# A two-layer graph attention kernel: the tail of its attention written by hand, its gates as SILU on ACT, and rows of its output stage loaded ahead

## What is computed

```python
def gt_layer(x, ntype, etype, src, dst, Wk, Wq, Wv, Wa, Watt, Wmsg, pri, skip, g, b):
    k, q, v = (typed_linear(x, ntype, W).reshape(n, H, HS) for W in (Wk, Wq, Wv))
    kT = einsum('nhd,htdo->nhto', k, Watt)
    vT = einsum('nhd,htdo->nhto', v, Wmsg)
    a = einsum('ehd,ehd->eh', kT[src, :, etype], q[dst]) * pri[:, etype].T / SQRT_D
    att = edge_softmax(a, dst, n)
    hag = segment_sum(vT[src, :, etype] * att[:, :, None], dst)
    h = silu(typed_linear(hag, ntype, Wa))
    alpha = sigmoid(skip[ntype])[:, None]
    h = h * alpha + x * (1.0 - alpha)
    return layernorm(h) * g + b          # 8 heads of 16; 16 node types, 32 edge types
out = layernorm(x + (gt_layer(gt_layer(x)) @ ff_w + ff_b))
```

## Time and profile before

| | us |
|---|---|
| median of 3 runs | 3545.18 (3544.02 to 3546.11) |
| profiled execution, its own time | 3543.11 |
| its span in the profile | 3541.3 |
| DVE busy | 2760.1 (78%) |
| PE busy | 2444.9 (69%) |
| POOL busy | 2417.9 (68%) |
| ACT busy | 1910.8 (54%) |

### The profile page before, as it was taken

The page is one execution under the profiler, slowest core; times in us unless marked ns, Lnnn a source line. Parts: engine busy times, 40 slices in busy tenths (PEclk is TensorE's granted clock), DMA queues, the critical chain, the costliest instruction groups (busy, mean ns, idle before and its releaser), DMA issues.

```text
span 3541.3 us, 62787 instructions
## 1 busy us (share of the span) xinstructions
PE 2444.9 (69%) x14287; PEld 1787.5 (50%) x14288; DVE 2760.1 (78%) x6215; ACT 1910.8 (54%) x4886; POOL 2417.9 (68%) x2501
## 2 busy tenths in 40 slices
PE   2777787477667676777677777657667676767765
PEld 1333333366656665666333333346556666666643
DVE  7667677488888888897687888758888787888765
ACT  1666677155445445555576777615445454455555
POOL 3666675577777777773566666477777777777746
PEclk8889998588898989988799999868888888888866
DMA  7999999755555555555799999965555555555350
GB/s 153 399 390 390 379 380 407 250 152 154 151 156 151 152 149 144 147 147 156 193 408 383 389 375 371 412 181 145 146 143 144 144 144 143 145 142 149 95 154 34
DMA packets 331225, 783.39 MB, mean 221 GB/s; under 512 B 87275, under 2 KB 262267, under 8 KB 318335
## 3 DMA queue, kind: packets, MB, share of 16 engines
q0 software_dynamic: 106016, 638.52, 50.7%
q1 hardware_dynamic: 216371, 139.98, 15.0%
q10 hardware_dynamic: 8448, 0.53, 0.2%
HBM read 335.84 MB, written 573.22 MB: 257 GB/s over the span
## 4 chain that ended last, share of the span: by engine, by line
issue 21%; DMA 19%; POOL 18%; DVE 15%; PE 10%; DVEq 9%; ACT 6%; POOLq 1%; SPq 0%; ACTq 0%
POOL region L838 15%; DMA relation_table<-region,scatter_node 13%; DVEq L1901 5%; PE bank L1182 4%; DMA region<-relation_table,key_of 3%; ACT region L925 3%; DVEq L1909 2%; DVE region_q L1879 2%; DVE region L1894 2%; PE bank L1350 2%; DMA region_q<-sums_by_node,gather_node 1%; PE bank L1212 1%; POOL region_q L741 1%; POOLq L831 1%; DVE arena L1884 1%
## 5 line engine op out<-in xcount | busy, mean ns | idle before, releaser
L838 POOL DMA_INDIRECT region<-relation_table,key_of x1568 | 1513.6, 965 | 500.9 <-issue 446.9
L1350 PE MATMUL bank<-region,arena 128*128 128x136 f32 x3968 | 700.3, 329 | 289.8 <-DVE region L1894 157.8
L1350 PEld LDWEIGHTS bank<-region,arena 128*128 128x128 f32 x3968 | 602.8, 226 | 371.5 <-issue 202.2
L925 ACT COPY region<-bank 128x512 f32<-128x512 f32 x1152 | 621.5, 601 | 290.1 <-DMA relation_table<-region,scatter_node 168.9
L1696 DVE COPY region<-bank 128x512 f32<-128x512 f32 x896 | 585.4, 685 | 210.5 <-DMA relation_table<-region,scatter_node 118.4
L1182 PE MATMUL bank<-sums,arena 128*128 128x512 bf16 x2048 | 618.2, 414 | 176.7 <-ACT region L925 142.4
L1061 ACT ACTIVATE arena<-iota_free,minus_dst 128x128 f32<-128x128 f32 x1984 | 629.4, 387 | 153.1 <-PE bank L1350 144.5
L1338 PE MATMUL bank<-region_q 128*128 x3968 | 632.4, 313 | 77.7 <-DVE region_q L1879 54.1
L1338 PEld LDWEIGHTS bank<-region_q 128*128 128x128 f32 x3968 | 596.0, 229 | 84.3 <-issue 84.1
L1870 DVE TENSOR_TENSOR bank<-bank,region 128x512 f32<-128x512 f32 x496 | 345.5, 697 | 292.4 <-issue 177.6
L1079 ACT ACTIVATE bank<-arena 128x256 f32<-128x256 f32 x62 | 24.0, 387 | 911.5 <-DVE arena L1989 911.5
(11 more groups left out here) (303 smaller groups left out, 2911.5 us busy)
## 6 DMA issues: line engine op xcount, KB each, us to landing
arena<-edge_places SPq DMA_DIRECT2D x496, 128.0 KB
region<-relation_table,key_of POOLq DMA_INDIRECT x1568
arena<-segment_flags SPq DMA_DIRECT2D x124, 128.0 KB
region_q<-q_rows SPq DMA_DIRECT2D x6, 768.0 KB, 16.0
aggregated_rows<-one_less_alpha SPq DMA_DIRECT2D x17, 256.0 KB
region<-aggregated_rows SPq DMA_DIRECT2D x16, 272.0 KB, 3.0
sums<-relation_weight_parts SPq DMA_DIRECT2D x32, 128.0 KB, 10.0
x_sorted<-arena SPq DMA_DIRECT2D x16, 256.0 KB, 14.7
```

The costliest lines, as they stand in the source:

```text
L838: pool.indirect_dma_start(out=rows[:, r, s], out_offset=None, in_=table, in_offset=bass.IndirectOffsetOnAxis(ap=key_of[:, n:n + 1], axis=0 ...
L925: nc.scalar.copy(stage[:, r, :, k * HS:(k + 1) * HS], bank[TABLE_BANK + k % TABLE_BANKS][:, :].rearrange("p (t o) -> p t o", t=RT)).then_i ...
L1350: ins = nc.tensor.matmul(bank[SUM_BANK[place_of(block_, q, SUM_RING)]][:, 0:SUMC], onehots[:, at, s], weighed_rows[:, weighed_at, s, :], s ...
```

## The change

It has three parts, and some lines that follow from them.

- The number of quads becomes 244. Block 30 has four, and behind its last product DVE, ACT and PE run a `tail` that is written out: the same helpers in an order of their own. In the tail DVE makes the marks of every second quad from 233 on, with one operation of 128x512 and a semaphore of its own. The last block keeps its differences in the unused half of `score` and its exponentials in the bank of the q rows. The count of early tiles in layer 0 is read by SP instead of POOL.
- ACT's gate is SILU of z. DVE's operation that opened the gate goes in both stages, `half_alpha` becomes `alpha_of_tile`, and `z_used` is replaced by `silu_done` or `var_ready`. In the table stage of layer 1 DVE's variance and centring of the first groups move.
- The first eight groups of h and x rows are loaded as soon as the last quad is weighed, before SP waits for the stored sums, and ACT scales those of h before its first step; the first eight transfers of aggregated rows have the ring's semaphore for themselves.

```diff
-NQUADS = NBLOCKS * QPB
+NQUADS = EDGE_QUADS + NTILES - 1
+LAST_BLOCK = NBLOCKS - 1
+TAIL = (LAST_BLOCK - 1) * QPB
+DVE_MARKS = range(TAIL + 1, NQUADS, 2)
...
+        def below_of(block_):
+
+            return score[:, 1 - block_.par] if block_.known and block_.b == LAST_BLOCK else below_max[:, :, :]
+
+        def exp_bank(block_):
+
+            return Q_BANK[0] if block_.known and block_.b == LAST_BLOCK else EXP_BANK
...
-            return 48 * (g // RING) + 48
+            return 48 * (g // RING) + 16
...
-                    for into, rows_ in ((o_in, agg_dram), (o_res, h_sorted), (o_x, x_sorted)):
-                        sp.dma_start(into[:, k], group_rows(rows_, g)).then_inc(rows_loaded[k], 16)
-
+                    sp.dma_start(o_in[:, k], group_rows(agg_dram, g)).then_inc(rows_loaded[k], 16)
+                    if g >= RING:
+                        for into, rows_ in ((o_res, h_sorted), (o_x, x_sorted)):
+                            sp.dma_start(into[:, k], group_rows(rows_, g)).then_inc(rows_loaded[k], 16)
+
+                sp.wait_ge(weighted, L * NQUADS)
+                for g in range(RING):
+                    for into, rows_ in ((o_res, h_sorted), (o_x, x_sorted)):
+                        sp.dma_start(into[:, g], group_rows(rows_, g)).then_inc(early_rows, 16)
                 sp.wait_ge(agg_stored, AGG_DONE)
...
-                    sp.wait_ge(sums_early, 1)
+                    early_done = sp.value_load(slots_done[0:1, 0:1], min_val=FIRST_LATE, max_val=NQUADS)
+                    sp.wait_ge(sum_added, early_done)
+                    sp.sem_inc(passed, 1)
...
-                    wait(act, z_used, tile.g)
-                    nc.scalar.activation(g_th, by_tile(bank[IN_BANK]), ACT.Tanh, scale=0.5).then_inc(tanh_done, 1)
+                    wait(act, var_ready, tile.g)
+                    nc.scalar.activation(g_th, by_tile(bank[IN_BANK]), ACT.Silu).then_inc(silu_done, 1)
...
+                for g in range(RING):
+                    scale_o_res(g)
                 for i in range(-3, GROUPS + 2):
...
                     if real(i + 3):
-                        scale_o_res(i + 3)
+                        if i + 3 >= RING:
+                            scale_o_res(i + 3)
                         gate(i + 3)
...
+                def tail():
+
+                    for n in range(TAIL, NQUADS):
+                        if n == TAIL:
+                            block_exponentials(Block(0, LAST_BLOCK - 1))
+                        if n == TAIL + 5:
+                            block_exponentials(Block(0, LAST_BLOCK))
+                        block_, q = pair(n)
+                        exponentials(block_, q)
...
+                        if n not in DVE_MARKS:
+                            mark(block_, q)
...
+                    for q in range(4):
+                        turn_maxima(last, q)
+                        sum_quad(*pair(TAIL + 1 + q))
+                    for n in range(TAIL + 5, TAIL + 8):
+                        sum_quad(*pair(n))
+                    spread_rescale(last)
+                    for n in range(TAIL + 8, NQUADS):
+                        sum_quad(*pair(n))
...
-                def open_gate(tile):
-
-                    z = bank[IN_BANK][:, :].rearrange("p (t d) -> p t d", t=GROUP)
-                    wait(dve, hn_ready, tile.g)
-                    dve.wait_ge(tanh_done, tile.g + 1)
-                    v.scalar_tensor_tensor(g_h, g_th, 1.0, z, ALU.add, ALU.mult).then_inc(z_used, 1)
-
...
-                        chain.step(v.scalar_tensor_tensor(hh[:, t], hh[:, t], half_alpha[:, g * GROUP + t:g * GROUP + t + 1], res[:, t],
+                        chain.step(v.scalar_tensor_tensor(hh[:, t], g_th[:, t], alpha_of_tile[:, g * GROUP + t:g * GROUP + t + 1], res[:, t],
...
+                    if l and tile.j == 2 and late.real:
+                        add_res(late, 0)
+                    if l and tile.j == 3 and late.real and tile.n >= 0:
+                        variance(late)
+                    if l and tile.n == 0:
+                        centre(early)
                     if l and tile.j == 0 and early.real:
                         scale(early)
-                    if l and tile.j == 2 and late.real:
-                        add_res(late, 0)
-                    if l and tile.j == 3 and late.real:
-                        variance(late)
...
                     if l and tile.j == 2 and late.real:
                         add_res(late, 1)
+                        if tile.n < 0:
+                            variance(late)
                     if tile.real:
                         evict(tile, DVE_HEADS[6:])
-                    if l and tile.j == 3 and late.real:
+                    if l and tile.j == 3 and late.real and tile.n != -1:
                         centre(late)
...
-                    z = bank[Z_BANK[g % 2]][:, :].rearrange("p (t d) -> p t d", t=GROUP)
                     hh, res = o_h[:, g % 3], o_res[:, g % RING]
...
-                    v.scalar_tensor_tensor(hh, o_th[:, g % 2], 1.0, z, ALU.add, ALU.mult).then_inc(z_used, 1)
...
+                def mark(n):
+
+                    dve.wait_ge(sum_psum, l * NQUADS + n - (ONEHOT_RING - 1))
+                    v.scalar_tensor_tensor(onehots[:, n % ONEHOT_RING], bc(iota_free[:, :], 1, QUAD), -1.0,
+                                           bc(minus_dst[:, n * QUAD:(n + 1) * QUAD], 2, P), ALU.mult, ALU.is_equal).then_inc(dve_marked, 1)
+
+                def tail():
+
+                    before, last = Block(0, LAST_BLOCK - 1), Block(0, LAST_BLOCK)
+                    find_maxima(before, 4, 0)
+                    find_maxima(before, 4, 1)
+                    tail_add(TAIL - 2)
+                    tail_weigh(TAIL)
+                    find_maxima(last, 0, 1)
+                    find_maxima(before, 4, 3)
+                    tail_add(TAIL - 1)
+                    find_maxima(last, 0, 3)
+                    scale_crossing(before.b, tail_tile(TAIL))
+                    find_maxima(last, 0, 0)
...
+                    for n in range(TAIL + 9, NQUADS):
+                        tail_weigh(n)
+                        tail_add(n - 1)
+                    tail_add(NQUADS - 1)
...
-                for at in range(2 + TURN * TURNS, NBLOCKS + 1):
+                for at in range(2 + TURN * TURNS, NBLOCKS):
                     block_of(Block(0, at))
-                for q in range(FIRST_ADDED):
-                    step(Block(0, NBLOCKS + 1), q)
+                tail()
```

165 lines of the change are left out of this document (113 added, 52 removed).

## The result

| | before | after |
|---|---|---|
| median, seven runs each | 3545.18 us (3542.47 to 3547.93) | 3528.16 us (3517.81 to 3532.21) |
| profiled execution, its own time | 3543.11 | 3517.81 |
| its span | 3541.3 | 3516.0 |

The ratio is 0.9945, interval 0.9936 to 0.9954: faster by 17.0 us in the medians and inside the forecast range. The profiled execution of after is its fastest run; five later runs gave 3522.48 (3522.15 to 3523.67; kernel before beside them 3545.08), 22.6 us faster. The seven runs of after spread more than the others: three took 3517.81 to 3522.06 us and four 3528.16 to 3532.21, and none of the five later ones came near the four. No profile of one of the four exists, so what made them longer stays open, and so do 5.7 us of the first median.

The account below looks back on a forecast made before the run. It took table stores, POOL's gathers in attention and an output loop of POOL and DVE, sometimes waiting for TensorE, as bounds. 11.9 + 3.7 + 2.5 + 1.4 + 8 = 27.5 us off 3545.2 gave 3517.7, range 3505 to 3532.

Parts of the forecast that it names:

- (c): Attention and output stage: the changes cancel, leaving little more than layer 0's drain, within 0.2%; chance 0.04.
- (d): Gates: SILU's tables lack COPY or IDENTITY, so every gate switches there and back, 82 us more, 3600; chance 0.04.
- rival (a): Output stage: TensorE sets it, so the loop gains 1.8 us and the ramp nothing, 3525; chance 0.17.
- rival (b): Layer 0's drain: TensorE's sums, 2.4 us a quad, hold it, not ACT; gain 7.8 us, 3522; chance 0.12.
- Layer 0's tail: End of layer 0's attention: four empty quads go and DVE takes six marks from ACT, gaining 11.9 us.
- lower bound: Layer 0's tail: dropping four empty steps saves 13.4 us less 5.6 that stays, 7.8 us for certain.
- part of it ACT's pace, which goes. I keep 6.5: Layer 0's tail: of the old drain's 11.8 us of DVE idle time, 6.5 stay, giving a 31.8 us tail.
- The argument that ACT has no gap: Layer 0's old drain, against rival (b): at its end ACT starts a mark every 1.95 us, back to back.
- Layer 1's stores: Layer 1's late tile stores: they follow POOL's earlier ones without a gap, 3.1 us sooner and faster, gaining 3.7 us.
- Start of the table stage: Second table-building stage: moved variance and centring of the first groups on DVE gain 2.5 us, from 0 to 5.
- Ramp: Output stage's start: 2.1 from early rows + 1.4 from two gates - 1.28 table load - 0.8 scaling = 1.4 us.
- Loop: Output stage, 13 periods: one DVE operation less shortens periods by 0.73 us, between 1.8 and 13 in all, taken as 8.

Follow-up runs that it names:

- e1: The changed kernel again with nothing edited: 3522.48 us, ratio 0.9941.
- e3: The changed kernel with two idle matmuls on TensorE behind each sum of the tail but the last: 3523.24 us, ratio 0.9944.
- e7: The changed kernel with idle TensorE matmuls before the output stage's first transpose and behind each group's input transposes: 3517.0 us, ratio 0.9927.
- e2: The changed kernel with all marks of the tail back on ACT: 3519.73 us, ratio 0.9934.
- e12: The changed kernel with later tail weighings further ahead and only quads 239, 241 and 243 marked on DVE, one add earlier: 3514.55 us, one run.
- e11: The kernel before, unedited, for a second profile: 3543.84 us, one run.
- e4: The changed kernel with the early loading and scaling of h and x rows undone: 3523.06 us, ratio 0.9943.
- e5: The changed kernel with the TANH gate and DVE's gate operation back in both stages: 3529.42 us, ratio 0.9965.
- e10: e7 with all marks on ACT and idle TensorE matmuls at the start of layer 1's table stage: 3509.6 us, ratio 0.9894.
- e13: e10 with the tail of e12: 3507.95 us, ratio 0.9893.

## Why the prediction was right, and where its steps were not

The range held the result and the rivals (c) and (d) fell. The forecast value was 10.5 us too low for the first median and 4.8 for the second, which lie nearer to the 3525 of rival (a) and the 3522 of rival (b). Rival (a) is not what happened, though: loop and ramp gave 5.4 and 3.7 us where it has 1.8 and 0. Its reason, TensorE, is there in the long periods. By the terms, with both profiles of before and, for the tail and the stores, the seven with the change's own tail (after, e1, e3 to e7):

- **Layer 0's tail, 11.9 forecast, 8.9 measured** (47.3 less a mean of 38.3). Its lower bound, 7.8 for four empty steps, holds nearly all of it. The step that failed is "part of it ACT's pace, which goes. I keep 6.5": DVE's work came as forecast (24.23 against 25.3), but 12.2 us of idle time stayed, as much as the old drain's 11.8. e2 shows that taking the marks off ACT brought nothing, and in the rows above a DVE mark as placed has a wait of its own behind it. The argument that ACT has no gap holds only from 1671.33 on: just ahead of it ACT had waited 6.08 us for DVE's scans; e12 shows that ACT's pace does go where DVE's marks stand early enough. Rival (b)'s number (7.8) was nearer than mine; its reason, TensorE's sums, fell with e3, apart from what a low clock may add.
- **Layer 1's stores, 3.7 forecast.** The mechanism is there, the gap of 3.39 is gone, but the gap was a matter of the run: e11 has 0.83. From the last gather to the last store, before took 71.1 and 68.5 us, the seven a mean of 69.3: 0.5.
- **Start of the table stage, 2.5 forecast, 0 at its end.** The first store came 1.7 us sooner at a low clock and 4.4 at a high one, but I let it count in full though the earlier trace rows have the DMA engines at 0.96 of the stage: the very cover that I gave to the rest of DVE's work. The last store did not move.
- **Ramp, 1.4 forecast, 3.7 measured** (last store to third power: 32.6 and 32.9 before, 28.9 and 29.0 after). The rows gave 2.1 (e4) and two gates 1.4 (e5), both as worked out. The two deductions failed: the table load (1.28) is hidden by ACT's wait for TensorE, and the scaling (0.8) ended 8.28 us before ACT's first copy, because SP's transfers began 26.4 us ahead of the last store of sums (3329.97 against 3356.40) and not the 17.6 of my estimate.
- **Loop, 8 forecast, 5.4 measured** (103.7 less 98.3; 6.7 in after's profile). The short periods fell by 0.65 (7.71 to 7.06), near the 0.73 of the sum and at POOL's 7.0. Long periods stayed, in changing number, for the reason named: the granted clock. What would have given the 8 and more is e7's and e10's.
- **Not forecast: 1.8.** From the last table store of layer 1 to the first gather of its attention, before took 13.9 and 14.0 us, the seven 11.7 to 12.5. Nothing was tried on it.

8.9 + 0.5 + 0 + 3.7 + 5.4 + 1.8 = 20.3 us, beside 17.0 and 22.6 by the medians. The total is nearer to the forecast than its terms: four gave 11.3 us less than forecast in all, and it was luck that the ramp and the term that I left out gave 4.1 more. Without them it would still lie above the range's low gain of 13.3.

## What to carry to other kernels

Before moving work off an engine that looks full, ask where in the other engine's order it will stand: six marks that wait behind an add cost at least as much as they relieved, and three marks one add earlier took 2.4 us off the tail. And look at what an engine waited for just before it ran without a gap. Where a loop has long and short periods, compare the same matmul in both: if its duration has two values, idle TensorE work that nothing reads may be worth as much as the instructions saved (17 to 23 us faster than before became 26 with it, and 36 and 37 with more of it and the tails of e2 and e12). A lead at the start of a stage paced by its DMAs should be costed at nothing.

## What the runs showed that was not expected

- SILU does not share its table with EXP here. After has four table loads of 1283 ns where before had one. Two of the three new ones end inside ACT's waits for TensorE, and the third (L1113) holds DVE for 0.98 us in a stage that POOL paces, so none shows in the time. The groups of loads in after:

```profile
L919 ACT ACT_TABLE_LOAD x1 | 1.3, 1283 | 33.7 <-issue 33.7
L985 ACT ACT_TABLE_LOAD x1 | 1.3, 1283 | 0.0
L1113 ACT ACT_TABLE_LOAD x1 | 1.3, 1283 | 73.1 <-DVE arena L2066 73.1
L1064 ACT ACT_TABLE_LOAD x1 | 1.3, 1283 | 0.0
```

- The same filler held TensorE's clock through the start of the table stage in e10 and not in e13, though TensorE was nearly as busy before (15.80 and 15.18 of 22 us). The clock of such a seam isn't set reliably by idle work alone.
- The table stages wander by several us with the same code: layer 0's took 536.3 to 541.7 us from first to last store over 14 profiles. Terms of 2 us in them can't be read from a pair of profiles.
